# Fp16 keys made group by group, and TensorE's program for groups 3 to 20 as a loop of nine passes

## The reference

```
q, k, v = (x Wq^T + bq), (x Wk^T + bk), (x Wv^T + bv)     as [b, channel, position]
k  = causal_conv(k, k_kernel) + k_D * k                   one 512-tap filter per channel
kv = k * v
y  = (causal_conv(kv, ssm_kernel) + D * kv) * q
x  = layernorm(x + y Wo^T + bo)
h  = square(relu(x Wfc^T)) ;  z = h Wproj^T               256 -> 1024 -> 256
x  = layernorm(x + spikes(z) / 5)                         five steps of a threshold neuron, counted
```

## Time and profile before

| | us |
|---|---|
| median of 3 runs (lowest, highest) | 899.39 (898.63, 899.83) |
| the profiled execution | 902.56 |
| its span, first to last instruction | 900.8 |
| PE busy | 753.9 (84%) |
| DVE busy | 778.5 (86%) |
| ACT busy | 517.2 (57%) |
| POOL busy | 400.9 (45%) |

### The profile page before, as it was taken

How to read it: one execution, slowest core, us unless ns; L and a number is a source line. 1 busy time by engine, 2 the same in 40 slices (tenths; PEclk the granted TensorE clock), 3 DMA queues, 4 the chain that set the end, 5 groups by cost and what they waited for, 6 DMA issues and landing times.

```text
span 900.8 us, 26648 instructions
## 1 busy us (share of the span) xinstructions
PE 753.9 (84%) x11392; PEld 554.1 (62%) x11392; DVE 778.5 (86%) x1157; ACT 517.2 (57%) x560; POOL 400.9 (45%) x307
## 2 busy tenths in 40 slices
PE   0078978788878988867469999999999999999993
PEld 0078978788778988867445555555545555555541
DVE  6887889887878789999757899999999999999885
ACT  2396666666665666633335656555666555666562
POOL 0352112222222222211346876666876666786542
PEclk9999999999998899976669999999999999999997
DMA  9985888876878787676110011111011111001001
GB/s 336 335 218 146 205 197 190 195 187 159 199 181 190 182 190 154 144 167 181 48 48 1 1 48 47 47 47 47 0 47 47 47 47 47 21 26 48 24 23 47
DMA packets 55614, 101.59 MB, mean 113 GB/s; under 512 B 5728, under 2 KB 41440, under 8 KB 53600
## 3 DMA queue, kind: packets, MB, share of 16 engines
q1 hardware_dynamic: 54144, 97.94, 41.7%
q10 hardware_dynamic: 1376, 2.23, 0.7%
HBM read 89.92 MB, written 27.01 MB: 130 GB/s over the span
## 4 chain that ended last, share of the span: by engine, by line
PE 38%; DVE 31%; POOL 15%; issue 12%; DMA 3%; ACT 1%; SPq 1%; POOLq 0%; DVEq 0%; ACTq 0%
PE ps L725 13%; POOL arena L671 13%; PE ps L747 12%; DVE arena L1211 7%; PE ps L842 5%; PE ps L849 4%; DVE arena L1055 2%; DVE u_maxima L943 2%; DVE arena L1168 2%; DVE arena L1208 2%; PE ps L823 2%; DVE arena L1187 2%; DMA arena<-kpad_dram 2%; DVE arena L1193 1%; DVE arena L996 1%
## 5 line engine op out<-in xcount | busy, mean ns | idle before, releaser
L501 ACT ACTIVATE arena<-arena 64x3584 f16<-64x3584 f16 x60 | 191.3, 3189 | 124.2 <-DVE arena L1035 123.5
L725 PE MATMUL ps<-arena 128*128 128x96 f16 x3072 | 147.6, 213 | 68.7 <-DVE arena L996 50.7
L747 PE MATMUL ps<-arena 128*128 128x64 f16 (+2 forms) x5088 | 151.7, 184 | 43.4 <-issue 23.7
L725 PEld LDWEIGHTS ps<-arena 128*128 128x128 f16 x3072 | 142.1, 102 | 71.7 <-issue 60.2
L671 POOL TENSOR_TENSOR arena<-arena 128x512 f16<-128x512 f32 x128 | 178.9, 1429 | 14.7 <-ACT arena L553 14.2
L747 PEld LDWEIGHTS ps<-arena 128*128 128x128 f16 x5088 | 147.3, 99 | 46.3 <-issue 40.6
L849 PE MATMUL ps<-arena 128*128 128x512 f16 x768 | 173.2, 379 | 2.8 <-POOL arena L671 2.8
L842 PE MATMUL ps<-arena 128*128 128x512 f16 x768 | 170.8, 379 | 0.9 <-issue 0.9
L635 POOL TENSOR_TENSOR arena<-arena 128x512 f16<-128x512 f32 x32 | 40.4, 1262 | 278.9 <-ACT arena L507 278.9
L1200 DVE TENSOR_TENSOR arena<-arena 128x512 f32<-128x512 f32 x128 | 137.7, 1129 | 10.4 <-POOL arena L671 9.0
L549 ACT ACTIVATE arena<-ps,read_factor 128x512 f32<-128x512 f32 x128 | 87.9, 687 | 79.4 <-PE ps L842 62.4
(11 more groups left out here) (106 smaller groups left out, 868.1 us busy)
## 6 DMA issues: line engine op xcount, KB each, us to landing
arena<-kpad_dram SPq DMA_DIRECT2D x166, 256.0 KB, 5.2
kpad_dram<-ksplit_dram SPq DMA_DIRECT2D x64, 256.0 KB, 5.6
qy<-in_uT SPq DMA_DIRECT2D x8, 1024.0 KB, 17.3
arena<-in_u SPq DMA_DIRECT2D x16, 512.0 KB, 4.2
out<-arena SPq DMA_DIRECT2D x16, 512.0 KB, 3.0
qy<-kpad_dram SPq DMA_DIRECT2D x22, 256.0 KB, 6.5
arena<-in_k SPq DMA_DIRECT2D x2, 512.0 KB, 4.8
ksplit_dram<-arena ACTq DMA_DIRECT2D x2, 512.0 KB, 3.7
```

Source lines behind the costliest of these rows:

```text
L501: nc.scalar.activation(*shifted(windows1_of(s, half)), ACT.Copy).then_inc(c1_copied, 1)
L725: last = nc.tensor.matmul(o, u16[:, x, t, tok:tok + P], wcur[:, r, w, t], start=(k == 0), stop=(k == 3 * DT - 1))
L747: last = nc.tensor.matmul(out[:, ch * COL + delta * B:(ch + 1) * COL], win[:, delta * P:(delta + 1) * P], data(xp, ch)[:, 0:cols], start=( ...
```

## The change

Three things change together.

Keys: DVE writes each quarter as fp32 into `kbuf`, which holds two whole chunks. The split is no longer made for a quarter of a chunk but for a group: in step g ACT and POOL split the keys of group g+1, all 16 sequences of 8 channels, into `k16`, now two groups in size. Before the first step one such split is made where there were four. `ktmp` is gone.

Weights: `wcur` is a single buffer. DRAM weights land in `wnext`, and DVE copies `wnext` to `wcur` after it has read the last quarter of a chunk. `project` of a chunk's first quarter waits for this copy (`wcur_ready`).

PE's program: groups 0 to 2 and 21 to 31 are written out. Groups 3 to 20 are a loop of nine passes of two groups. The quarter that is projected differs between even and odd passes, so each of the two `project` calls is there twice in the loop, behind a branch on the pass's parity. ACT's loop is now written out.

```
-    ktmp_ready; k16 = part(16, ...); wcur = part(1.5, ... r=2 ...); ktmp = part(4, F32, ...)
+    kbuf = part(16, F32, "p (r q n) -> p r q n", r=2, q=GPC)
+    wcur = part(0.75, F16, ...); wnext = part(0.75, F16, ...); k16 = part(4, F16, "p (r a n) -> p r a n", r=2, a=2)
...
     SP, at s % GPC == 0
-                    sp.wait_ge(proj, GPC * (chunk - 1))
-                    load_w(chunk, chunk % 2)
+                    sp.wait_ge(wcur_ready, 2 * (chunk - 1))
+                    load_w(chunk, wnext, ld_wnext)
...
     ACT
+            def k_part(g):
+                act.wait_ge(proj_read, GPC * (g // GPC + 1))
+                if g >= 2:
+                    act.wait_ge(c1_half, 2 * (g - 2) + 2)
+                nc.scalar.activation(by_quarter(k16[:, g % 2, 0]), keys_of(g), ACT.Copy).then_inc(k_hi, 1)
...
     POOL, step(s, base, more)
-                if more:
-                    k_part(s % GPC, (s // GPC + 1) % 2, base + s + GPC)
+                if not (isinstance(base, int) and base + s == NG - 1):
+                    k_part(s + 1, base + s + 1)
...
     DVE, read_projection
-                if not isinstance(n, int) or n >= 2:
-                    dve.wait_ge(k_lo, n - 1)
...
+                if quarter == GPC - 1 and chunk + 1 < NC:
+                    dve.wait_ge(ld_wnext, 16 * (chunk + 1))
+                    nc.vector.tensor_copy(wcur, wnext).then_inc(wcur_ready, 2)
...
     PE
+            def conv1(s, g):
+                pe.wait_ge(k_lo, g + 1)
...
+            def pair_of_steps(first, nth):
+                g = first + 2 * nth
+                with pe.If(nth % 2 == 0):
+                    project(first % GPC, g + GPC)
+                with pe.Else():
+                    project((first + 2) % GPC, g + GPC)
+                conv1(first, g)
+                conv2(first - 1, g - 1)
+                with pe.If(nth % 2 == 0):
+                    pe.wait_ge(wcur_ready, nth + (first + 1) // 2 + 2)
+                    project((first + 1) % GPC, g + 1 + GPC)
+                with pe.Else():
+                    project((first + 3) % GPC, g + 1 + GPC)
+                conv1(first + 1, g + 1)
+                conv2(first, g)
+            LOOPED = range(3, QUERY_UNTIL + 1)
+            for g in range(LOOPED.start):
+                step(g)
+            with pe.Fori(0, len(LOOPED) // 2) as nth:
+                pair_of_steps(LOOPED.start, nth)
+            for g in range(LOOPED.stop, NG):
+                step(g)
```

More of the change, by code:

```diff
@@ L216, in build @@
             sem(n) for n in ("c1_copied_dve", "c1_half", "c2_half", "c2_widened"))
-        ld_wcur = [sem(f"ld_wcur{r}") for r in range(2)]
-        proj, proj_read, ktmp_ready, k_hi, k_lo = (sem(n) for n in ("proj", "proj_read", "ktmp_ready", "k_hi", "k_lo"))
+        ld_wcur, ld_wnext, wcur_ready = (sem(n) for n in ("ld_wcur", "ld_wnext", "wcur_ready"))
+        proj, proj_read, k_hi, k_lo = (sem(n) for n in ("proj", "proj_read", "k_hi", "k_lo"))
         kv_ready, kv_hi, kv_lo, y_ready = (sem(n) for n in ("kv_ready", "kv_hi", "kv_lo", "y_ready"))
@@ L501, in copy_windows, with step @@
                 nc.scalar.activation(*shifted(windows1_of(s, half)), ACT.Copy).then_inc(c1_copied, 1)
[L503 to L506, removed]
+            def step(s, g):
+                if g + 1 < NG:
+                    copy_windows(s + 1, g + 1, 0)
+                act.wait_ge(kv_ready, g + 1)
                 nc.scalar.activation(kv16[:, s % 2, 0], vbuf[:, s // GPC, group_of(s):group_of(s) + GC], ACT.Copy
                                      ).then_inc(kv_hi, 1)
-                if more:
-                    k_part(s % GPC, (s // GPC + 1) % 2, base + s + GPC)
[L511 to L524, removed]
+                if g + 1 < NG:
+                    k_part(g + 1)
+                if g + 1 < NG - GPC:
+                    copy_windows(s + 1, g + 1, 1)
+            for half in range(2):
+                copy_windows(0, 0, half)
+            k_part(0)
+            for g in range(NG):
+                step(g % PAIR, g)
             def y_turn(i):
@@ L626, in _, with k_part @@
                                            ).then_inc(u_max_done, 1)
[L628 to L631, removed]
+            def k_part(s, g):
+                pool.wait_ge(k_hi, g + 1)
+                nc.gpsimd.tensor_tensor(by_quarter(k16[:, s % 2, 1]), keys_of(s), by_quarter(k16[:, s % 2, 0]),
+                                        ALU.subtract).then_inc(k_lo, 1)
             def step(s, base, more):
@@ L647, in _ @@
                 split_u(n)
-            for quarter in range(GPC):
-                k_part(quarter, 0, quarter)
+            k_part(0, 0)
             phase1(pool, step)
@@ L713, in _, with project @@
         def _(pe):
-            def project(quarter, r, n, banks=PA, before=0):
+            def project(quarter, n, banks=PA, before=0):
                 if not isinstance(n, int) or n > before:
@@ L776, in conv2 @@
                 convolve(1, PC2[:, s % 2], lambda a, ch: kv16[:, s % 2, a, ch * COL:(ch + 1) * COL],
-                         lambda half, c, a: windows2_of(g, half)[:, c // 2, c % 2 * 2 + a],
+                         lambda half, c, a: windows2_of(s, half)[:, c // 2, c % 2 * 2 + a],
                          g + 1, c2_half)
[L780 to L787, removed]
-                    pe.wait_ge(proj_read, GPC)
-                conv1(s, g, base + (s // GPC + 1) * GPC)
-                if not first:
-                    conv2((s - 1) % PAIR, g - 1)
@@ L793, in _, with step @@
-            for s in range(PAIR):
-                step(s, 0, True, 0, s == 0)
-            for pair in range(1, NC // 2):
-                for s in range(PAIR):
-                    step(s, pair * PAIR, pair < NC // 2 - 1 or s < GPC, pair)
-            conv2(PAIR - 1, NG - 1)
+            def step(g):
+                if g < NG - GPC:
+                    if g % GPC == 0:
+                        pe.wait_ge(wcur_ready, 2 * (g // GPC + 1))
+                    project(g % GPC, g + GPC, PA, int(g == 0))
+                if g == 0:
+                    pe.wait_ge(proj_read, GPC)
+                conv1(g, g)
+                if g:
+                    conv2(g - 1, g - 1)
@@ L1001, in read_projection @@
                 dve.wait_ge(proj, n + 1)
[L1002 to L1003 removed]
                 tiles = banks.rearrange("p i (b x) -> p x (i b)", b=4)
[L1005 removed]
+                for s, dst in ((0, kbuf[:, r, quarter]), (1, quarter_of(vbuf[:, r], quarter)),
                                (2, quarter_of(qy[:, bass.ds(chunk * CH * COL, CH * COL)], quarter))):
```

45 lines of the change are left out of this document (20 added, 25 removed).

## The result

The changed kernel takes 904.70 us, the median of five runs (902.95 to 907.19), against 899.39 before (five runs, 898.63 to 903.47); the ratio is 1.0049, with a 95% interval of 1.0025 to 1.0072. It is slower by 4 to 5 us (4.4 by the ratio, 5.3 by the medians), where 2.2 were forecast.

What follows compares the result with a forecast made beforehand. PE's code packets (5.07 us each) set the pace, a DVE-POOL port limit close by; 2.5 + 0.4 + 7.6 - 11.8 + 3.5 = +2.2 us gave 904.8 us profiled, 901.6 median; range 889 to 912.

Steps and rivals of the forecast that it cites:

- Steady part, -11.8: Sixteen steps between `times_v` of groups 5 and 21: 10.85 us each instead of 11.59, so -11.8 us.
- the case of the earlier trace: Steady steps as seen around group 26 before: DVE's copies begin ahead of POOL's work, 10.69 us a step.
- the rival "circle": Steady part: POOL stays ahead of DVE's copies, ACT, POOL and DVE hold each step at 11.37 us; 909.9 us, 18%.
- The rival "faster": Steady part: POOL works while DVE reads PSUM, 9.93 us a step as in group 10; 886.9 us, 15%.
- First pass, +7.6: Loop's first pass on PE: all 6.0 packets of code must come, 30.4 us against 22.8, +7.6 us.
- Start and other copies, +2.9: Fifth projection waits for DVE's copy of weights, 2.5 us late; six more weight copies, two outside the steady part, 0.4 us.
- the bounds of the first pass: Limits for the loop's first-pass cost: 0 to 10 us, the upper with three more for a PE clock dropping after idleness.
- Tail, +3.5: Steps 28 to 30 get a split of keys they lacked: 2.9 us on DVE plus 0.6 for late `times_q`, 3.5 us.
- Groups 21 to 27: Written out on PE as before, they were to stay at the pace of the code packets, with no term.
- the signs to look for: Changed profile: later first convolution, no packets within the loop's later passes, `times_v` of groups 3 to 5 8 us further apart.
- The loop not held: PE's loop: every pass fetches 6.0 packets anew, 30.4 us against 21.7, eight times +8.7; about 971 us, 8%.

Runs made afterwards that it cites:

- Experiment 1: Changed kernel with PE's loop written out for all groups again, keys by group and single weights buffer kept: 908.8 us, ratio 1.0124.
- experiment 6: Changed kernel with 96 matmuls of never-run code put ahead of PE's loop: 909.97 us, ratio 1.0109.
- experiment 2: Changed kernel with ACT doing the high parts of `kv` and keys ahead of the first window copy: 888.45 us, ratio 0.9907.
- experiment 3: Kernel before the change, with ACT's high parts of `kv` and keys put ahead of the first window copy: 899.28 us, ratio 1.001.
- experiment 5: Changed kernel with 96 matmuls of never-run code at the end of the loop's body, behind a branch never taken: 1053.29 us, ratio 1.17.

## Why the prediction was right, and where its sizes were off

**The mechanism.** Slower by a little, as a difference of large terms, was forecast, and so it came. Experiment 1 shows that the stalls were code, the queue's rows and experiment 6 that the loop is held, and experiment 2 that the steady pace hangs on when POOL starts, beside DVE's masks and copies or ahead of them.

**Steady part, -11.8.** Measured 173.83 - 185.38 = -11.55, a step of 10.86 us for 10.85. The number is nearer than its reasoning, and that is in part luck. The prediction took every step for the case of the earlier trace rows, POOL behind the copies, 10.69 us, with 0.15 for small things. The runs show this case in every second step (10.64 us). In the others POOL comes ahead of the copies, as in the rival "circle" (11.37), and from that start to the next it is 11.13 us on average. PE waits for POOL's split in seven of the sixteen steps and not in every one.

**The rival "faster"** was rightly named (9.93 us a step) and wrongly tied to chance. What keeps POOL out of DVE's reading of PSUM isn't luck of phase: it is one window copy of 3.19 us that ACT does ahead. Experiment 2 moved it, and the steps are 9.73 us.

**First pass, +7.6.** Measured 39.94 - 35.16 = +4.8 for the three steps with it, +4.3 against experiment 1 (35.60): the term was too high by 2.8 us. PE in the changed kernel, at the loop's first projection, at its longest stall and at the first projection of the second pass:

```profile
105.97 3.95 PE L725 MATMUL ps<-arena 128*128 128x96 f16 x89
...
129.38 2.73 PE L747 MATMUL ps<-arena 128*128 128x48 f16 x79 [3.90 <-issue]
...
135.40 4.25 PE L725 MATMUL ps<-arena 128*128 128x96 f16 x96 [0.30 <-issue]
```

And the same two projections, of groups 3 and 5, before:

```profile
100.85 5.62 PE L725 MATMUL ps<-arena 128*128 128x96 f16 x96
...
124.36 4.25 PE L725 MATMUL ps<-arena 128*128 128x96 f16 x96 [0.20 <-DVE qy L1016]
```

The pass took 29.4 us on PE, for 30.4 forecast, and the same matmuls took 23.5 before, for 22.8: +5.9. Between 102.4 and 134.4 us the packets came 4.6 us apart on average, a little faster than the 5.07 that the prediction took. Another 1.0 us came back right behind the pass: from the second of these projections to `times_v` of group 5 it is 6.78 us instead of 7.75, since PE no longer waits for code there. The prediction had said that nothing hides the term. The jumps over a branch's other half are waited off inside the stalls, the longest of them 3.9 us.

**Start and other copies, +2.9.** This term was too low by 2.4 us: the first `times_v` is 4.27 us late and that of group 2 5.29. The start of phase 1 on PE, changed kernel, kernel of experiment 6, and before:

```profile
72.27 5.77 PE L725 MATMUL ps<-arena 128*128 128x96 f16 x96 [2.21 <-DVE arena L1037]
83.23 7.04 PE L725 MATMUL ps<-arena 128*128 128x96 f16 x96 [2.70 <-DVE qy L1030]
```

```profile
71.16 4.25 PE L725 MATMUL ps<-arena 128*128 128x96 f16 x96 [2.21 <-DVE arena L1040]
80.60 5.86 PE L725 MATMUL ps<-arena 128*128 128x96 f16 x96 [2.70 <-DVE qy L1033]
```

```profile
78.96 5.86 PE L725 MATMUL ps<-arena 128*128 128x96 f16 x96 [2.70 <-DVE qy L1016]
```

The wait itself was priced well. The copy of weights took 0.25 us (0.2 was taken), and the fifth projection began at 72.27, 2.7 us late (2.5 forecast), of which 0.4 us were there already when the fourth began. What was left out is the clock: the prediction has it only in the bounds of the first pass. Behind the new idle time of 2.21 us the same 96 matmuls took 5.77 us at a granted clock of 0.71; in experiment 6 they took 4.25 at 1.00. Of the six kernels with this wait three show the long form (5.77 to 5.86) and three the short one (4.25), one execution each. That is 1.5 us of the 4.27. The next 1.2 us are the projection at 83.23, 7.04 instead of 5.86. Its idle time of 2.70 us was there before the change too, and over all kernels it takes 5.5 to 7.0 us, in experiment 3, which has no new wait, 6.94. So this part is variation between executions and not shown to be the change's.

**Tail, +3.5.** Measured 32.16 - 28.71 = +3.45. Steps 28 to 30 took 10.02, 10.90 and 11.24 us instead of 8.95, 9.07 and 10.69, and DVE is busy 3.3 us longer in them. Groups 21 to 27 were to cost nothing and gave -0.35.

**Not priced: the passage to phase 2.** `times_v` of group 31 is 1.6 us late, the end 3.4. Where DVE meets POOL after it, changed kernel:

```profile
446.59 2.34 POOL L665 TENSOR_TENSOR arena<-arena 128x1024 f32<-128x1024 f32 x1 [7.09 <-issue]
447.05 4.04 DVE L1174 SCALAR_TENSOR_TENSOR arena<-arena,w_scale 128x2048 f16<-128x2048 f32 x1 [4.80 <-ACT arena L584]
```

and before:

```profile
444.33 2.35 DVE L1156 SCALAR_TENSOR_TENSOR arena<-arena,w_scale 128x2048 f16<-128x2048 f32 x1 [3.93 <-ACT arena L583]
444.66 4.22 POOL L665 TENSOR_TENSOR arena<-arena 128x1024 f32<-128x1024 f32 x1 [7.01 <-issue]
```

Before, DVE came first and its work was 2.35 us; now POOL comes first and it is 4.04. From `times_v` of group 31 to the end it is 473.2 and 473.3 us in the two kernels with the old keys, and 474.1 to 476.1 in all eight with keys by group. So the loss goes with the new data path; that this meeting is its cause was not tested.

**The sum** by what was measured: +5.3 to group 2, +4.8, -11.55, -0.35, +3.45, +1.8 behind group 31 = +3.4 us, the difference of the spans. Two terms were wrong by more than 2 us in opposite directions (start 2.4 too low, first pass 2.8 too high), so that the forecast lies nearer than its terms deserve, and that is luck; the 1.8 us at the passage, which no term had, are what is left. Of the signs to look for, the first pass was the one that failed: some 8 us more were to lie between `times_v` of groups 3 and 5, and it is 4.8 from group 2 to 5 and 1.3 from 3 to 5.

**The loop not held** (8%) did not come, but experiment 5 shows how near it was. The prediction counted seven packets for the body and one fetched behind it, and this fits: with one more each pass took 39.6 us, where that rival had feared 30.4 for six. The eight are counted from the program; the nine are measured. The Trainium skill (Runtime: NRT & Kernel Launch, section Instruction fetch mechanics) gives two sizes, a buffer of 128 KiB on PE and two lines of 16 KiB that are held. The first agrees with these runs (eight packets of 16 KB held, nine not), the second doesn't.

## What to carry to other kernels

A stall that the profile calls "issue", at a constant distance of instructions and with packets on the instruction queue beside it, is code; a loop on that engine removes it if the whole body, with all branches that it jumps over and the packet behind it, fits into what the engine holds. Count these packets before, since one too many costs far more than the loop can bring. When a stall goes, look for the next meeting point: here the change alone cost some 4 us and the new order alone brought nothing, and both together gained 8 to 11 us against before (experiment 2, by the ratio and by the medians).

## What the runs showed of the hardware

- PE held eight packets of code of 16 KB (2048 instructions), by the count of the program, and not nine: with eight in a loop none came in 158 us, with nine in a loop nine came in every pass, and the kernel took 149 us longer. That all nine come fits giving up the oldest first; only these two sizes were run.
- A packet took 5.07 us at a DMA share of 77%, and still about 4.4 at 46%, with gaps of some 4 and 6 us while nothing else was on the queues. So the other DMAs explain little of it; I had expected them to explain most. What does is not shown.
- A gap of 2.21 us on PE was followed in three executions by 96 matmuls in 5.77 to 5.86 us (granted clock 0.70 to 0.71) and in three by the same in 4.25 (1.00).
- Where DVE's copies and POOL's subtractions started together, both were stretched: two copies from 2.22 to 3.18 us, a subtraction from 1.16 to 2.15. Where POOL started first, DVE's masks and first copies were. Over sixteen steps DVE was busy 18 us longer than with POOL beside the reading of PSUM (169.81 against 151.35).
